# Adaptive-norm transformer stack on one core: Gelu of the feed-forward gate read from PSUM block by block

## What is computed

```python
def ffn_layer(x, g, bln, W1, b1, W2, b2):
    mu = x.mean(-1, keepdims=True)
    var = ((x - mu) ** 2).mean(-1, keepdims=True)
    xn = (x - mu) / jnp.sqrt(var + 1e-05) * g + bln
    hg = xn @ W1 + b1                     # 2 * 341 columns
    a, gate = jnp.split(hg, 2, -1)
    return a * jax.nn.gelu(gate, approximate=False) @ W2 + b2
...
for i in range(DEPTH):                    # DEPTH = 6
    x = attn_layer(shift_tokens(x), Wqkv[i], q_scale[i], k_scale[i], Wo[i]) + x
    x = ffn_layer(shift_tokens(x), ln_g[i], ln_b[i], W1[i], b1[i], W2[i], b2[i]) + x
```

## Time and profile before

| | us |
|---|---|
| median of 3 runs (3195.01 to 3196.76) | 3195.43 |
| the profiled execution, device time | 3194.76 |
| its span, first to last instruction | 3192.9 |
| PE busy | 2894.4 (91%) |
| DVE busy | 2485.8 (78%) |
| ACT busy | 2424.9 (76%) |
| POOL busy | 2059.5 (65%) |

### The profile page before, as it was taken

The page is one execution under the profiler, slowest core; times in us unless marked ns, Lnnn a source line. Parts: engine busy times, 40 slices in busy tenths (PEclk is TensorE's granted clock), DMA queues, the critical chain, the costliest instruction groups (busy, mean ns, idle before and its releaser), DMA issues. The chain is left out here.

```text
span 3192.9 us, 91014 instructions
## 1 busy us (share of the span) xinstructions
PE 2894.4 (91%) x34796; PEld 2022.6 (63%) x34988; DVE 2485.8 (78%) x3265; ACT 2424.9 (76%) x3708; POOL 2059.5 (65%) x1410
## 2 busy tenths in 40 slices
PE   8288887799999999999999999999899999999996
PEld 6166766566666666666666666666666666666662
DVE  3788886778787888788888788888788888888872
ACT  3366665688887878887878787878787878787872
POOL 0355654777776777767777677777677776777760
PEclk9688988899999999999999999999999999999997
DMA  1000001110001100001000011000010000100002
GB/s 46 11 24 21 21 23 33 30 43 20 20 20 27 48 20 20 20 20 55 20 20 20 17 30 47 20 20 20 25 49 20 20 20 17 34 22 21 20 20 60
DMA packets 80517, 84.66 MB, mean 27 GB/s; under 512 B 23734, under 2 KB 53908, under 8 KB 79668
## 3 DMA queue, kind: packets, MB, share of 16 engines
q1 hardware_dynamic: 79988, 82.40, 9.7%
q0 software_dynamic: 448, 1.20, 0.1%
HBM read 22.72 MB, written 2.10 MB: 8 GB/s over the span
## 5 line engine op out<-in xcount | busy, mean ns | idle before, releaser
L1333 POOL TENSOR_TENSOR qk_r<-qk_r,qk_t 128x1024 f32<-128x1024 f32 x384 | 917.1, 2389 | 569.5 <-DVE qk_r L1189 381.1
L807 PE MATMUL pa<-w_hi,xs_hi 128*128 128x512 f32 x1152 | 580.3, 504 | 73.0 <-DVE w_lo L1269 42.2
L1182 DVE TENSOR_REDUCE ss<-sq 128x16 f32<-128x1024 f32 x384 | 462.7, 1205 | 9.1 <-ACT sq L991 8.7
L1189 DVE TENSOR_TENSOR qk_r<-pa,rot 128x1024 f32<-128x1024 f32 x384 | 465.3, 1212 | 0.0
L1198 DVE TENSOR_TENSOR qk_t<-pa,rot 128x1024 f32<-128x1024 f32 x384 | 465.3, 1212 | 0.0
L807 PE MATMUL pa<-w_hi,xs_lo 128*128 128x512 f32 x1152 | 458.2, 398 | 0.0
L807 PE MATMUL pa<-w_lo,xs_hi 128*128 128x512 f32 x1152 | 456.4, 396 | 0.0
L835 PEld LDWEIGHTS px<-ident_sb,qk_r 128*128 128x128 f32 x3072 | 354.6, 142 | 141.5 <-issue 97.5
L1044 ACT COPY kT<-px 64x1024 f32<-64x1024 f32 x384 | 385.0, 1003 | 72.0 <-PE px L835 67.3
L835 PE MATMUL px<-ident_sb,qk_r 128*128 128x128 f32 x3072 | 404.4, 275 | 15.1 <-ACT oT L1061 10.3
L1342 POOL TENSOR_TENSOR qk_r<-qk_r,inv 128x1024 f32<-128x1024 f32 x192 | 370.5, 1930 | 43.8 <-ACT inv L1028 43.4
(11 more groups left out here) (155 smaller groups left out, 5306.0 us busy)
## 6 DMA issues: line engine op xcount, KB each, us to landing
pT<-prT SPq DMA_DIRECT2D x768, 64.0 KB, 2.0
w_raw<-in_Wqkv SPq DMA_DIRECT2D x6, 1536.0 KB, 6.6
s_x_turn<-c_xn SPq DMA_DIRECT2D x32, 128.0 KB, 2.0
s_x<-c_xn SPq DMA_DIRECT2D x32, 128.0 KB, 2.0
wo<-in_Wo SPq DMA_DIRECT2D x6, 512.0 KB, 4.6
c_x_ring<-in_x SPq DMA_DIRECT2D x32, 64.0 KB, 1.8
o_x<-in_x SPq DMA_DIRECT2D x8, 256.0 KB, 4.8
out<-o_out SPq DMA_DIRECT2D x8, 256.0 KB, 4.3
```

Source lines behind the costliest of these rows:

```text
L807: last = pe.matmul(pa[(u + c) % 2][:, half * 512:half * 512 + 512], x[:, j * P:(j + 1) * P], w[:, at], start=(k == 0), stop=(k == 2))
L1182: dve.reduce_sum(ss[:, c, :], heads(sq[:]), AX.X).then_inc(s[sum_sem], 1)
L1189: dve.tensor_tensor(heads(qk_r[:, j % 2, c, :]), heads(pa[(3 * j + c) % 2][:]), per_head(rot[:, 2 * c, :]), ALU.mult).then_inc(s[cos], 1)
L1333: pool.tensor_tensor(qk_r[:, j % 2, c, :], qk_r[:, j % 2, c, :], qk_t[:, c, :], ALU.add)\
```

## The change

`gelu` is gone. The three bias passes of a group become three Gelu passes of the same shapes, each straight from `pg` with its bias into `gt`. The load of Gelu's table set now stands ahead of the first of them, at the head of slot 1, and the load of the Exp and Ln set behind the last. The semaphore `gelu_done` is dropped: `gated` waits for `gate_out` instead.

```diff
-                def gate_bias(i, k):
+                def gate_gelu(i, k):
                     g, live = group(i, 2)
                     if live:
                         m = HBLK[k][1]
                         act.wait_ge(s["gate_done"], 3 * g + k + 1)
-                        act.activation(gt[0:m, k, :], pg[0:m, :], ACT.Identity, bias=b1[0:m, 1, k:k + 1])\
+                        act.activation(gt[0:m, k, :], pg[0:m, :], ACT.Gelu, bias=b1[0:m, 1, k:k + 1])\
                             .then_inc(s["gate_out"], 1)
 
-                def gelu(i):
+                def tables(i, name):
+
                     g, live = group(i, 2)
                     if live:
-                        act.wait_ge(s["gate_out"], 3 * g + 3)
-                        act.activation(gt[:], gt[:], ACT.Gelu).then_inc(s["gelu_done"], 1)
-                        act.preload_act_table_set(EXP_LN)
+                        act.preload_act_table_set(name)
...
                     for j in range(GT):
                         if j == 1:
-                            gate_bias(i, 0)
+                            tables(i, GELU)
+                            gate_gelu(i, 0)
                         square_q(i, j)
                         copy_qT(i, j)
                         if j == 1:
-                            gate_bias(i, 1)
+                            gate_gelu(i, 1)
...
                         copy_kT(i, j)
                         if j == 1:
-                            gate_bias(i, 2)
-                            gelu(i)
+                            gate_gelu(i, 2)
+                            tables(i, EXP_LN)
                         exponentials(i, j)
...
-                        if k == 0:
-                            dve.wait_ge(s["gelu_done"], g + 1)
+                        dve.wait_ge(s["gate_out"], 3 * g + 3)
                         dve.wait_ge(s["a_done"], 3 * g + k + 1)
```

More of the change, by code:

```diff
@@ L48 @@
 EXP_LN = "natural_log_exp_and_others"
+GELU = "gelu_and_others"
 def wait_for(eng, sem, count):
@@ L682, in stack @@
             wo_done res_attn fs_ready center_done fc_ready fsq_ready var_done fln_done frs_ready fn_mul fn_ready
-            gate_done gate_out gelu_done a_done h_ready w2_done res_ready""".split()
+            gate_done gate_out a_done h_ready w2_done res_ready""".split()
         s = {n: sem(n) for n in names}
```

## The result

The changed kernel takes 3234.85 us (median of 4 runs, 3231.78 to 3238.47) against 3196.1 us before (median of 4, 3195.01 to 3197.84): ratio 1.0121, 95% interval 1.0104 to 1.0139. It is 1.2% slower, with less work in it. In the profiled execution the span grew from 3192.9 to 3230.7 us, by 37.8.

The account below looks back on a forecast made before the run. Each group was taken as bound by ACT up to `copy_oT`, then PE; +1.27 - 0.36 = +0.91 us over 46 groups gave +41.9, less the edges +39.4, hence 3234.8 us. Forecast range 3217 to 3244, widened to 3214 to 3252.

Parts of the forecast that it names:

- What bounds the kernel: Each group: an ACT path up to `copy_oT` in slot 1 (1536.62), then a PE path from `transpose_q` (1536.76).
- The load's price, +1.27: Head of slot 1: the load delays the first gate pass and PE's `gate_block(1)` by 1.27 us per group, nothing covering it.
- What comes back, -0.36: Entry of slot 2: with the large Gelu gone, PE's transposes can start 0.36 us sooner after `a_block(1)`, per group.
- The period: One full group: +1.27 - 0.36 = +0.91 us, so 53.1 instead of 52.2 us.
- The two entries: PE's entry to `gate_block(1)` in slot 1, +1.27 us, and to slot 2's transposes, -0.36 us.
- The edges: Two draining groups gain 2 us together (between 0 and 3.0); idle time in first groups of a few layers gives 0.5 us.
- ACT's busy time: Sign in the profile after: ACT's busy time falls by about 71 us while the span grows.
- The load hides: Rival: ACT reaches the head of slot 1 with 0.91 us or more to spare, load vanishes; 3176 us, chance 0.10.
- the two halves cancel: Rival: load about half hidden and PE's gain larger than 0.36 us; 3189 to 3202 us, chance 0.05.
- Nothing comes back: Rival: PE loses 1.27 us without winning 0.36, something unseen holding slot 2's entry; 3251 us, chance 0.08.
- A switch costs more than its row: Rival: a load before a pass PE waits for costs twice its 1.28 us; 3294 us, chance 0.02.

Follow-up runs that it names:

- the run without the Gelu: Kernel before with the large Gelu left out of the computation, both table loads staying behind the bias passes; 3174.67 us, ratio 0.9937.
- The run with the moved load: Kernel before with only the load of Gelu's set moved to the head of slot 1, the large Gelu kept; 3232.05 us, ratio 1.0113.
- the second load: Changed kernel with one more table load (Exp and Ln set) ahead of the first gate pass; 3308.72 us, ratio 1.0355.
- the third: Changed kernel with two more table loads ahead of the first gate pass; 3458.67 us, ratio 1.0821.

## Why the prediction was right

Point by point, by the steps of the prediction.

*What bounds the kernel.* An ACT path up to `copy_oT`, then a PE path. Confirmed from both sides: taking 1.49 us from ACT in front of `copy_oT` gained 0.41 us per group, taking 4.05 gained no more. That `gated`'s wait for the Gelu was no prize is shown by the run without the Gelu, where it is gone and 0.41 us of period are all that is won.

*The load's price, +1.27.* Measured +1.27 at `gate_block(1)`, of which 1.18 are shown as idle time. The claim that PE was held there already, which no row marked as idle, is borne out: from the start of the pass to `gate_block(1)` it is 0.74 us in the changed kernel (1539.98 to 1540.72), where PE plainly waits, and it was 0.74 before. That the hold was 0.06 us rests on an assumed overlap and was not measured; what is measured is that no slack covered the load.

*What comes back, -0.36.* Measured -0.36 between `a_block(1)` and the transposes. The run with the moved load shows that it comes back for a reason that has nothing to do with the Gelu: PE arrives late at `copy_oT` and no longer waits there. The prediction booked the 0.36 under the removed Gelu. In the sum that is the same; as an account of causes the moved load is right and the prediction loose. The change as a whole is the load's delay minus a wait that the delay itself overtakes.

*The period*, +0.91, was +0.86 to +0.87. The two entries make 0.91; the rest of the cycle, from the transposes of slot 2 to the next `gate_block(0)`, has 38.06 us of the new period where it had 38.11 of the old. The prediction let PE run head to tail there. The rows show one more wait, at `transpose_k` of slot 2, whose first weights come from POOL (`norm_k`), which in turn had waited 0.45 us for ACT's `inverse_norms`. Its row in the kernel before, then this wait over the whole run, before and after:

```profile
1540.06 0.86 PEld L835 LDWEIGHTS px<-ident_sb,qk_r 128*128 128x128 f32 x8 [0.24 <-POOL qk_r L1342]
```

```profile
PEld px L835 <- POOL qk_r L1342: 18.9, 52, 2.4
```

```profile
PEld px L836 <- POOL qk_r L1342: 7.5, 6, 2.4
```

46 of these waits are gone, one for each full group, and from `transpose_k` to `down` PE takes 0.87 us instead of 0.90 to 0.92. That is most of the 0.05, and it is gone as well in the run without the Gelu, where 0.41 and not 0.36 were won. So ACT's late stream held PE at two places of slot 2, by 0.36 us and by some 0.04 more, and the prediction had only the first.

*The edges.* From the first gate pass of the 46th group to the end it was 127.95 us before (3064.95 to 3192.9) and 125.83 after (3104.87 to 3230.7), a gain of 2.1 where 2 was expected. The five periods that lead over into a new layer grew by 0.61 to 0.79 us and not by 0.86, about 1 us in all where 0.5 was booked. The first gate pass of the run came 2.3 us later (671.77 and 674.03), of which the load explains 1.3; for the rest I have no cause. The load hides in the last group: ACT still stands idle for 0.87 us behind it.

```profile
3190.52 1.28 ACT L1077 ACT_TABLE_LOAD   x1
3192.67 0.69 ACT L1070 ACTIVATE gt<-pg,b 128x512 f32<-128x512 f32 x1 [0.87 <-PE pg L927]
```

The total, 3234.8 forecast and 3234.85 measured, agrees better than the terms deserve, and that is luck. The runs of the changed kernel spread over 6.7 us, the sum of the profiled execution was 1.6 us too large (+39.4 against +37.8), and the medians make up for it.

*ACT's busy time* fell by 59.6 us and not by 71. The removed Gelu alone makes 71.2. The durations of all ACT instructions, added up, fell from 2603.0 to 2532.8 us, by 70.2. But neighbouring passes overlap in the rows, and busy time counts an overlap once: 178.0 us of overlap before, 167.5 after. The passes of slot 2 that now wait for PE (idle 0.57 and 0.71 us there) stand apart where they ran head to tail, by about 0.1 us each.

*The rivals.* "The load hides" is refuted by PE's 1.18 us of idle time and by ACT's wait for the residual, which is still there in full (1.76 us, before 1.77): what ACT saves in one group is lost before the next. That the two halves cancel, with the load half hidden, falls with the same 1.18 us and with a gain of 0.41 and no more. "Nothing comes back" is refuted by the 0.86 us. "A switch costs more than its row" is refuted by 1.27 us for the load that was moved and 1.29 us for a further one, as long as the clock holds. The Trainium skill, page "ScalarE: Activation LUTs", section "What ACT_TABLE_LOAD costs", adds a drain of about 1.38 us to each load; in these traces a load follows its predecessor by 0.01 to 0.02 us, and what needs nothing from PE follows it as closely, so here the row alone is the price.

## What to carry to other kernels

Work that an engine issues for itself, such as a table load, has the price of the wait that stands behind its place: the same 1.28 us cost 1.27 us in one place and 0.15 us some passes further on. Before moving such a step, list for each possible place who waits for the next instruction and how much slack that wait has, and count from where the waiting engine would first wait, not from its first visible instruction. And an engine's busy time is no measure of such a change: this one took 60 us from ACT and cost 38.

## What the runs showed of the hardware

The clock of PE reacts to short pauses, and not always the same way. With pauses of 0.98 to 1.33 us ahead of `gate_block(1)` in the changed kernel the granted clock stayed at 1.00 behind all 46, and no product behind one was slow. With the second load (pauses of 2.26 to 2.62 us) it fell to 0.50 in 11 of 46 groups. With the third (3.55 to 3.90 us) it fell in all 46: in 41 during the pause, and then it stood at 0.50 (1.2 GHz of 2.4) for nearly 7 us, which cost about 2.4 us per group; in five, each the first of a layer, 0.6 to 1.4 us after `gate_block(1)` had started, for half as long, which cost 1.2 us. Each of these pauses follows the eight transposes of q. Whether these have a part in it, and what decides among equal pauses of 2.47 us, the runs do not show. The Trainium skill, page "TensorE: Matmul & The Clock Gate", section "Why this matters for your kernels", warns of idle gaps in the matmul stream that bring the clock back to half; the traces agree, with 0.50 near all pauses of 3.55 us and more and near some of 2.47 us.
